# One joined product for the division of two softmax heads by their row sums, and new merge orders of four streams on all four engines

## The reference

```
query = seq2 + b_self
key   = concat([seq1 + b_prev, seq2 + b_self]);  value = concat([seq1, seq2])
q, k, v = projections, 16 heads of 16
score_prev = q @ k[:, :l1]^T / 4  (keys past seq_len1 masked);  score_self = sum(q * k_self) / 4
weights = softmax(concat(score_prev, score_self))
cond = (weights_prev @ v_prev + weights_self * v_self) @ Wo + bo
for l in range(2):
    h = shift_token(x);  q, k, v = h @ wqkv[l], 8 heads of 64
    q, k = l2norm(q) * q_scale, l2norm(k) * k_scale
    q, k = rotary_xpos(q, k)
    attn = softmax(mask(8 q @ k^T))        # blocks of 128, each sees itself and the one before
    x = x + (attn @ v) @ wo[l]
    h = layernorm(shift_token(x)) * ln_g + ln_b
    a, g = split(h @ w1[l] + b1);  x = x + (a * gelu(g)) @ w2[l] + b2
out = x_in + x
```

## Time and profile before

| what | value |
|---|---|
| runs of the kernel | 3531.66, 3533.99, 3534.14 us; median 3533.99 |
| span of the profiled execution | 3530.7 us, 58337 instructions |
| PE busy | 3456.5 us (98%) |
| DVE, ACT, POOL busy | 2573.7 (73%), 2312.5 (65%), 742.2 us (21%) |
| chain that ended last | PE 88%, DVE 6%, ACT 4%, issue 2% |
| TensorE clock granted | 0.8 of full speed in the first two of 40 slices, 0.9 or more in the others |
| DMA | 99.56 MB, mean 28 GB/s |

### The profile page before, as it was taken

One profiled execution on the slowest core, in us unless ns is written; L12 is line 12 of the kernel. 1 busy time (PEld: TensorE's weight loads), 2 busy tenths in 40 slices (PEclk: granted clock), 3 DMA queues, 4 the chain that ended last, 5 costly groups with the idle time before them and its releaser, 6 DMA issues.

```text
span 3530.7 us, 58337 instructions
## 1 busy us (share of the span) xinstructions
PE 3456.5 (98%) x20452; PEld 2423.6 (69%) x20452; DVE 2573.7 (73%) x7101; ACT 2312.5 (65%) x5077; POOL 742.2 (21%) x882
## 2 busy tenths in 40 slices
PE   7899999999999999999999999999999999999997
PEld 4566776767776667777667777667767667767665
DVE  4577777777777777777777777777777777777764
ACT  2466766766766766766766766766666766666764
...
DMA packets 99201, 99.56 MB, mean 28 GB/s; under 512 B 9568, under 2 KB 97504, under 8 KB 98912
## 3 DMA queue, kind: packets, MB, share of 16 engines
...
q10 hardware_dynamic: 1360, 2.47, 0.2%
...
## 4 chain that ended last, share of the span: by engine, by line
PE 88%; DVE 6%; ACT 4%; issue 2%; DMA 0%; POOL 0%; SPq 0%; POOLq 0%; ACTq 0%; DVEq 0%
PE ps L1114 14%; PE ps L1009 12%; PE ps L1125 8%; PE ps L1090 6%; PE ps L1023 6%; PE ps L1080 5%; PE ps L1069 5%; PE ps L1058 4%; PE ps L924 4%; PE ps L914 3%; PE ps L897 3%; PE ps L1043 3%; PE ps L868 3%; ACT attn_area L746 3%; PE ps L860 2%; PE ps L949 2%
## 5 line engine op out<-in xcount | busy, mean ns | idle before, releaser
L625 POOL TENSOR_TENSOR inv<-ssq_f,minus_half 128x16 f32<-128x16 f32 x128 | 419.4, 3276 | 1057.2 <-DVE ssq_f L1320 1057.1
L746 ACT ACTIVATE attn_area<-attn_area,f_nb,inv 128x128 f32<-128x128 f32 (+1 forms) x1024 | 546.1, 536 | 117.4 <-DVE f_nb L1348 116.6
L1114 PE MATMUL ps<-feed_area,w_s 128*128 128x256 f32 x2560 | 606.1, 382 | 4.2 <-DVE feed_area L1383 3.7
L1114 PEld LDWEIGHTS ps<-feed_area,w_s 128*128 128x128 f32 x2560 | 467.4, 190 | 88.0 <-issue 25.4
L1257 DVE TENSOR_REDUCE c_mx<-ps 128x2 f32<-128x512 f32 x512 | 348.7, 687 | 134.5 <-PE ps L897 132.5
L699 ACT ACTIVATE cond_area<-ps 128x512 f32<-128x512 f32 x512 | 298.9, 592 | 62.4 <-PE ps L914 59.1
L1344 DVE CUSTOM_DVE_ANT_0 attn_area<-ps,cst 128x128 f32<-128x128 f32 (+1 forms) x1024 | 303.4, 351 | 43.3 <-issue 41.2
L1394 DVE SCALAR_TENSOR_TENSOR feed_area<-ps,b_s,feed_area 128x256 f32<-128x256 f32 (+1 forms) x448 | 213.7, 477 | 138.8 <-ACT feed_area L772 123.0
L1125 PE MATMUL ps<-feed_area,w_s 128*128 128x256 f32 x1280 | 293.9, 381 | 0.3 <-DVE feed_area L1394 0.3
L1359 DVE TENSOR_SCALAR attn_area<-attn_area,f_inv 128x128 f32<-128x128 f32 (+1 forms) x1024 | 258.0, 315 | 9.1
L470 DVE COPY attn_area<-ps 128x384 f32<-128x384 f32 x256 | 141.8, 554 | 165.5 <-PE ps L1069 165.4
...
## 6 DMA issues: line engine op xcount, KB each, us to landing
...
cond_area<-cond_area SPq DMA_DIRECT2D x128, 6.0 KB
...
```

The costliest lines, as they stand in the source:

```text
L625: nc.gpsimd.tensor_tensor(inv[:, l, t, :], ssq_f[:, l, t, :], minus_half[:, :], ALU.pow).then_inc(SL[l]["inv_norm"], 1)
L746: nc.scalar.activation(soft[:, h % SOFT, lo:hi], soft[:, h % SOFT, lo:hi], ACT.Exp, bias=f_nb[:, l, q, h:h + 1], scale=inv[:, l, q, h:h + ...
L1114: last = mm(ps[:, N0 + f % 2, c * N:(c + 1) * N], w1_s[:, l, k, lo:lo + P], hn[:, k, :], start=(k == 0), stop=(k == KD - 1))
```

## The change

The division of a pair of heads becomes one product. The row sums are kept per head, and the reciprocal writes each of them twice, so that a row of `f_inv` holds four values per head of which three (block 0 once, block 1 twice) scale three stretches of 128 elements. One product of 128x768, with `f_inv` broadcast, replaces the four scalings, and `probs_scaled` counts pairs of heads. The strings of all four engines in `ORDER`, `HEAD` and `TAIL` are new; the cuts, which say how far each stream lags, are as before. Lines behind the tables have a number higher by one.

```diff
 ORDER = dict(
     PE=((53, 19, 23, 0),
-        "SARARSNRARSRASASSRAANSARSASSNSSNSANSSNARSRSAAASRNSSSAARASNASAAAARNNSSANARASARARANRSAARNAASAASRAANSARS"
-        "ASASNRASSSANNRSASSAANAANASRSANANSASSANAARASASASARNAS"),
+        "SARNARSRRASRASASSRASAASASNRARRASSSNSAAASNAANARSASAASNANASSSRSSAANSNSAASNRRAANRRASANRSRNAASAASSANNSAR"
+        "ASASRASSSNANRNAASARNSSASNAAARSNASSSAAANSSAARASAASRAN"),
...
-    inv_sum=HP, probs_scaled=FH * 2, p_turned=FH, p_copied_act=len(ACT_TURNS), p_copied_dve=FH - len(ACT_TURNS),
+    inv_sum=HP, probs_scaled=HP, p_turned=FH, p_copied_act=len(ACT_TURNS), p_copied_dve=FH - len(ACT_TURNS),
...
-        f_sum = sb("f_sum", [P, DEPTH, TILES, FH])
-        f_inv = sb("f_inv", [P, DEPTH, TILES, FH])
+        f_sum = sb("f_sum", [P, DEPTH, FH, TILES])
+        f_inv = sb("f_inv", [P, DEPTH, FH, 2 * TILES])
...
-                    pe.wait_ge(SL[l]["probs_scaled"], upto(seq, "probs_scaled", 2 * h + 2))
+                    pe.wait_ge(SL[l]["probs_scaled"], upto(seq, "probs_scaled", h // 2 + 1))
...
-                    V.reciprocal(f_inv[:, l, :, 2 * p:2 * p + 2], f_sum[:, l, :, 2 * p:2 * p + 2]).then_inc(SL[l]["inv_sum"], 1)
+                    V.reciprocal(f_inv[:, l, 2 * p:2 * p + 2, :].rearrange("p h (q a) -> p h q a", a=2),
+                                 f_sum[:, l, 2 * p:2 * p + 2, :].rearrange("p h (q a) -> p h q a", a=1)
+                                 .broadcast_to([P, 2, TILES, 2])).then_inc(SL[l]["inv_sum"], 1)
                     dve.wait_ge(SL[l]["inv_sum"], upto(seq, "inv_sum", p + 1))
-                    for h in (2 * p, 2 * p + 1):
-                        for q in range(TILES):
-                            lo, hi = (0, P) if q == 0 else (P, 3 * P)
-                            V.tensor_scalar(soft[:, h % SOFT, lo:hi], soft[:, h % SOFT, lo:hi],
-                                            f_inv[:, l, q, h:h + 1], None, ALU.mult).then_inc(SL[l]["probs_scaled"], 1)
+                    both = soft[:, (2 * p) % SOFT:(2 * p) % SOFT + 2, :].rearrange("p h (c k) -> p h c k", c=3)
+                    V.tensor_tensor(both, both, f_inv[:, l, 2 * p:2 * p + 2, 1:4].rearrange("p h (c a) -> p h c a", a=1)
+                                    .broadcast_to([P, 2, 3, P]), ALU.mult).then_inc(SL[l]["probs_scaled"], 1)
```

More of the change, by code:

```diff
@@ L159 @@
     PE=(
[L160 to L162 removed]
+        "AAAAAAAAAAAAAAAAAAAAAAAAAAAAAAAAAAAAAAAAAAAAAAAAAAAAAAAAAARAARRARRARAARARAASRSRRAARAAAASASAAAAASASAS"
+        "AASAASSSAAASAAAASASAAASAAASAAASASAAASAAAASSASASASANARARAANRARRSARARARAANNSAARNAAARNANAARAARANASAANAA"
@@ L163 @@
+        "NSSSNASSARAASASSRASAARSSASAASARRAASSAAARSAASAASAARSAAASA"),
     DVE=(
-        "AAAAAAAAAAAAASARAAAAAAAAAAAAAAASAAAAAAAAAAAAAAAAAAAAAAAAAARAAAAARAARSRARARARARRAARAAAAASASAASAAAASSA"
-        "SAAAAASAASAAAARAASSSASAAAAASSSASSAAAARAASSSAAAAAAASANAARAAARARARNRRANAARNSRSARSAAARRNANAAANANASAASSA"
-        "ANNSSSAAASASAAASSAAASASANASAAARAASAARASAAASAARSSSAARRARSRSRAS"),
+        "AAASAAAAAAAAAAAAAAAAAAAAAAAAAAAAAAARAAAASAARAAAAAAAAAAAAAAAAAAAASRAAARRRARARAARRAAAAAASAASAAAAASAASA"
+        "SSRAASAASRSAAASAASAAAAAAAAAAAASSASASASRRAAASSSAASASAANAARSAAANRRRAARANNRARAANAARAARSANNAAAASANSAAAAS"
@@ L167 @@
+        "SNNSSASAAASSRSAASAAAASRSAAASASSARSRASAAARSSAARRAARRASAAAASNSA"),
     Activation=(
-        "AAAAAAAAAAAAAAAAAAAAAAAAAAAAAAAAAAAAAAAAAAAAAAAAAAAAAAAAAAARAARRARRAAARAAARSRAARSRRASRAAAASSSASAAASA"
-        "SAAAASAAAASAASAAASAASASAAAAASAASAAASASSSAAAASAAAAAAARNRARARNASSARARNRAANRSRANAARASRNASANARNSANAANAAA"
-        "SSSSSAAASASAARASAAARAASSRRARSAAAANSAASASAAAASSASRAASRAAARSSRRRASA"),
+        "AAAAAAAAAAAAAAAAAAAAAAAAAAAAAAAAAAAAAAAAAAAAAAAAAAAAAAAAAAARARAARRRAARARAARRSARASAARASAARASAAASAAAAA"
@@ L171 @@
+        "SSASASSASAASAAAAAAASSAAAAAAASSASAAASASASAASAASAASAARNAARARRASRAAAAANRRSARNAANNNRSARNAAARSAARANAASAAA"
+        "SNASASNRASAASSSASAARSAASASSARRNASAARSASAAARASASAASSSAAAARARARASRR"),
     Pool=(
-        "SAAAASAAAAASAAAAASAASAAAARAAASAAAAAAAASAAAAAAAAAARSRAASAAAAAASAAAAAASRARSSASSAAAAAASASAAAASRARASASAS"
-        "AAAASAASAAAASAAAAAAASAAASSAARRAASARSSASSARAAANASAAAARANSASRASARSAASRARAASAASARAAAAAAASNNASARNNRSAASN"
-        "ARRRSAAARSSASASAAAAASARNRSASAAASAAAAAANSAAAARARAASSSNNRASNASARRSSRAA"),
+        "SAAAAARAAAAAAASSAAAAASRSAAAASAAAAASAAAASAAASSAAASAAASASSARAAAAAAAAAAASAAAASRAAARRAASAAAASAASASSRAAAS"
@@ L175 @@
+        "AARAARRARASASAAAASAAARAASASAAASAAASAAAAAASAANSAARSNAAAASSASRARNAAAASAASRAAASRNSSAANAASRARRSAAAAASSAA"
+        "NASAARANASAANSARSAASAAAANNARAAARASSASANRSASRAASAAARNASARSSSASRAAASRR"),
 )
@@ L178 @@
     PE=(
-        "SARASRNARRSRASSSNRNNSSRRRSSSSNSSRNSNSSSSSRSSRSNSSNRNNRSRNRSRNSSRNNSSSSRSSSRSNRSSSSRNNSRSSSSRSNSSNRNN"
-        "RSRNRSNRSSNNSSSNSSSSNNNSNSNSSNSSSSSSNSSSRNRRSRRNRRNRSRNRRNRSNSNSSSSSSSSNSSNNSSSNSSSSSNSSNNNNNNNNNNNN"),
+        "SARARNSARRSRASSSNRSNNSRRSRSSSNSSRNSSNSSSSRSSNSNRSSNRNRSRNRSRNSSNSSRNSSRSSSSSSNRRNSRNSSRSSSSRSNSSNRNR"
+        "RNSRNSRNSSSSNNSNSSSSNSNNNSNSSNSSSSNSSSSSRNRRRSRNRSRRNRRNRNRSNNSSSSSSSSSNSNSSSNSSSNSSSNSSNNNNNNNNNNNN"),
     DVE=(
-        "SNRARRRRSRSNSSSSSNSRSSNSSNRSSRSSSSNNNSSRSSRNNSRSNRNRNSSRSSSSSSNSSNSRSSRNSSSRSSSNRNSNRSRRSRNRRNRNRSNS"
-        "RSNSNSSSSSNNSNSNSNSNSSSSSSSSSSRSNNNNSRRNSRRRRSNRNRRSNSSSSSSSNNANRSSSSSSSSSNNSSNNSSNNNNNNNNRNNNN"),
+        "SSRRNASNSSSSRSNSRSSRRRNSSNRSSSSSRNSSNRSSRNRRSNRRNSNNNSRSSRSSSSSSSNSSSRNSNSSSSNSRSNRSSRSRNRNNSNSRNRSR"
+        "NSSNSSSSNNSNRSSNRNNSRSSSSSSSSSSSRNSNNNRNRRRRSSRNRRRNNSSSSSSNSSNSSSNSSSSASNNSSNRSSSNNNNNNNNNNNNN"),
     Activation=(
-        "SNRSANSRSSSNRSSSSNSRNSRSRSSSNSSSSSNRSRNNSRNNRSRNRSSRNSRSNSSSSSSRSSNNSRRRSSSNSSSSRSNSSRNRRRNRNSSNRNNN"
-        "SSSSNNNSSNSSSNSNSSSSNSNSSSSSSRRRRSNNRNRRRNSRSRNSRNRSSSSNSSSSNSSNSNSSSNSNNSSSSSNNNNNSNNNNNNN"),
+        "RSNANSSRSSNSRRSSSSSNSNSRRSNSSSNSSSRSRNNNRSSNRRRNSSSRNSRSSSSSSNSSRRNNRSSRSSSNSSSSSRSNNNRNRSRSNRNRSRNS"
+        "NSSSSNSSSNSSSNNNNNSSNSNSSSSSSRNRSSRRRNRRRNSRRSRRNNSSSSNSSSSSSNSNSNNSNSSSSSNSSNNNSNNNNNNNNSN"),
     Pool=(
-        "NSSSRSSSSRSSNRRSRNNSSRNNASNRNRNSSSSSRRNRSSSRSNSSNSSRNSRNSRNNSRSNSSRRSANSSSSSSSRRRASNSNSSSARRSSRNNRNS"
-        "SNSNNNSSNNSNSARSNNSNSRSRNRNSNSNRRSNSSSNSASSSRRNSRNNNRNSRSNNNSSNRRSNNRNNRRSNSNSSSNSSSASNN"),
+        "NNSRRRNSRRNSRSRRSRNSSSNSRRSRNRSRSSNNSNNSNSSSNSNSASSSASSSSSRSRSSNSANRRSNSNRSNSNRRNRSSNNSRSSRNSSSSNSRR"
+        "SSNNASANSRNSSSNSNSNRSSNSNRSSSRSNNNRRNRNNRRNNRSSRSSSSNSNNSNSSSNSSSNRNNSNANNSSRNSSSARNRSNN"),
 )
```

15 lines of the change are left out of this document (7 added, 8 removed).

## The result

The changed kernel takes 3546.52 us (median of 6 runs, 3542.85 to 3549.44) against 3534.06 (6 runs) for the kernel before: a ratio of 1.0034, 95% interval 1.0023 to 1.0046. One of the six runs of the kernel before took 3614.13 us, in a slower state of the chip, and the ratio leaves it out. So the change is slower by a third of a per cent. 3539.5 was forecast, with a range of 3510 to 3562; the time lies in the range and in the 3530 to 3548 that the forecast was given as, but outside the 0.2% that was named with the same chance.

The account below looks back on a forecast made before the run. PE was taken as the bound, busy 106.06 of a 106.51 us pass. Terms -34.8 + 8.7 + 9.0 + 11.6 + 11.0 = +5.5 on 3530.7 gave 3536.2, plus 3.3 to the median: 3539.5 us, range 3510 to 3562.

Parts of the forecast that it names:

- four waits that go: PE's waits at `turn_probs(1,4)`, `mix` 0, `turn_max` 3 and `qk(1,1,1)` go in each pass: 15.4, 6.1, 7.0, 6.4 us gained.
- `mean(0,0)`: PE step moved up behind `out_proj(0,1)`; waits .31 a pass for DVE's and POOL's additions, 9.0 us.
- `score` 0: PE step waiting for the DMA that places the query's parts: 11.16 against 10.76 of PE work, .40 a pass, 11.6 us.
- `score` 2: PE step waiting for DVE's maximum of `score` 0: 0 to .38 a pass, upper end taken, 11.0 us.
- switches, ahead of a narrow step: PE changes between wide and narrow tiles, 27 a pass instead of 24, .10 each over 29 passes: 8.7 us.
- joined product, loop: DVE's one division product, about .96, makes the first head .4 later but PE work hides it: 0 us.
- head and tail: New strings before and after the main loop, with waits on long chains: 0 taken, 6 us to either side.
- What hides it: All but one first-head `turn_probs` have over 6.1 us of PE work behind `scores`, hiding the joined product: 0 us.
- The first: Rival: faster, the new waits at `mean(0,0)`, `score` 0 and `score` 2 don't come; 3508 us, half of them 3524; chance .32.
- The second: Rival: slower, ACT's table load ahead of `weigh(1,1)`'s eviction makes `out_proj(1,0)` wait; at .8 a pass 3562 us; chance .21.
- The third: Rival: slower, joined product late for two first heads, layers 0 and 1, .3 each a pass; 3556 us; chance .08.
- The fourth: Rival: slower, POOL's power of `rotate(1,0)` blocks the joined product, 1.64 a pass; 3587 us; chance .03.

Follow-up runs that it names:

- experiment 5: The kernel before with POOL's product of `own_key` issued earlier, at the place of `project` 2: 3514.62 us, ratio 0.9948.
- experiments 1 to 3: 1: changed kernel with old division, 3543.17 us; 2: old orders with joined product, 3567.23 us; 3: changed kernel with old strings of the tail, 3541.97 us.
- experiment 9: Kernel before with POOL's `own_key` product at `project` 2 and one 128x384 product per head replacing the scalings: 3514.98 us, ratio 0.9948.
- experiment 2: The changed kernel with the old orders of the kernel before, the joined product kept: 3567.23 us, ratio 1.0099.

## Why the prediction was right or wrong

The mechanism held: PE's waits of before went, and new ones came at the three places named, and at one more, with the joined product hidden in the loop. The sizes, over 29 passes, read from the starts of PE's rows in the two traces:

| term | forecast | measured |
|---|---|---|
| four waits that go | -34.8 | about -37, with the longer first matmuls behind them (none left in the pass; `turn_probs(1,4)` by itself .55 in experiment 5) |
| `mean(0,0)` | +9.0 | about +12 (.34 ahead of `mean` and .08 in the step itself) |
| `score` 0 | +11.6 | +6.2 |
| `score` 2 | +11.0 | +5.7 |
| `hidden(1,2)` | not named | +6.8 (.13, and .10 in the step itself) |
| switches, ahead of a narrow step | +8.7 | +7.6 (13 a pass instead of 10, .09 each) |
| switches, first matmul behind a narrow step | not named | +7.7 (.58 a pass instead of .31) |
| joined product, loop | 0 | 0 (-.65 without it) |
| head and tail | 0, with 6 to either side | -3.0 and +8.2 |

- *"So a switch costs .10."* This step failed. It priced only the gap ahead of a narrow step, and that price and the count of three more were nearly right. It left out the full-width step behind, whose first matmul is longer, and so the switches cost 15.3 instead of 8.7. No run changes the number of switches alone; the counts are from the traces.
- *The new waits.* The list has three, and `hidden(1,2)` is missing: the chain that feeds it, through the gating on ACT and DVE, does not stand in the prediction.
- *".21" for `mix` 0 and ".11" for `qk(1,1,1)`.* They were counted as waits. .06 of the first and all of the second are longer first matmuls, behind a narrow step and behind a wait; the first stays in the new order.
- *Head and tail at 0.* The tail was mis-sized by 8.2 us; with the head's -3.0 the two stay within the 6 us allowed. The sentence on what hides the joined product spoke of a pass only; in the tail it costs 4 to 5 us (experiments 1 to 3), and by experiment 9 the price there too is that the first head waits for both. Of the rest, which is the new strings', the cause stays open; the clock has a part in it.
- *"What hides it: every `turn_probs` of a pair's first head but one stands over 6.1 us behind its `scores`."* True of the new order, and there it was hidden. As a rule for the old one it would have been wrong: `turn_probs(0,4)` at 9.9 us and `(0,2)` had no slack (experiment 2). That their pairs stand late in DVE's and ACT's strings is the likely reason; no run shows it. The distance on PE says what cover there is, not what the other engines have queued in front.
- *`score` 0 and 2* were the right places at half the price: the placing took 11.21 us (1851.03 to 1862.24), as long as in the head, PE had 10.92 us of work in front where 10.76 was added up (the .10s again), and a longer wait at the first makes that at the second shorter.
- *Rivals.* The first did not come: all three new waits are there. The second neither: `out_proj(1,0)` has no wait. The third is what the joined product does in the old orders, not in the new. The fourth falls: 29 times in the loop the product begins while POOL's power runs, and takes its .96.

The prediction gave the same chance, .36, to 3530 to 3548 and to "within 0.2%", 7 us to either side; these are not the same, and the measured +12.5 lies in the one and outside the other. That the loop came out only 3.5 us over the forecast (+9.0 against +5.5) is in part luck: the waits at `score` were put 10.7 us too high, and the two terms not named make up 14.5.
